# A sparsemax attention with its engine queues reordered, and a quantised convolutional layer whose weights are prepared during the projection before it

## The chip, the cores and the metric

The kernel runs on one NeuronCore of a Trainium2 chip. The metric is the device time of one execution in microseconds (us). Five engines work side by side, each with its own queue of instructions taken strictly in order: TensorE (PE in the profile, its weight loads PEld), VectorE (DVE), ScalarE (ACT), GpSimd (POOL) and SyncE (SP), which issues the DMAs. They wait for one another through semaphores that only count up.

## The reference, cut to what matters

Eight layers are applied to 2 x 512 tokens of 256 numbers. Two of them are touched.

```python
# layer "L0_ffn": quantised up projection, convolution over tokens, SiLU, quantised down projection
h = bit_linear(x, w1)                     # 256 -> 1024; x to 8 bits per token, w to -1, 0, 1 by mean|w|
h = depthwise_conv1d(h.transpose(0, 2, 1), conv_w, conv_b)   # 3 taps along the tokens
h = jax.nn.silu(h.transpose(0, 2, 1))
x = x + bit_linear(h, w2)                 # 1024 -> 256; h to 8 bits by its largest |value| per token

# layer "L1_xattn": 16 heads of 16, 512 queries, 1024 keys
scores = einsum('bhqd,bhkd->bhqk', qh, kh) * scale
attn = sparsemax(scores)                  # max(scores - tau, 0), tau such that a row sums to 1
out = einsum('bhqk,bhkd->bhqd', attn, vh)
```

## The kernel before, in words

The program is a row of stages. A stage is a block in which each engine has its own list of instructions; all engines meet at its end, so whatever ends last in a stage sets when the next begins.

**The projection of layer 0** (`project_out`, stage `l0o`) multiplies `o_all` by `wo` for eight token tiles (L324, 16 PE instructions a tile) and VectorE adds each tile to `x` (L337). ScalarE does nothing there.

**The convolutional layer** (`bit_conv_ffn`, stage `f0`) loads its weights at its own start (L2282 to L2285), sums their sizes on ScalarE (L2294, L2297), normalises and rounds `x` on VectorE (L2371 to L2399), takes the weight scales (L2403 to L2405) and rounds both weights (L2414 to L2416). Eight channel chunks follow, each one VectorE chain: widen by the token's scale (L2423, two halves), three taps (L2430, L2431, L2432), then SiLU on ScalarE (L2311). Then all eight token tiles are transposed and their largest values taken (L2349, L2436), the scales are spread over the partitions (L2442, L2354, L2315), the eight chunks are multiplied and rounded (L2448 to L2450), and only then the down products run (L2362) and are added (L2453).

**Sparse attention** (`sparse_attention`, stage `l1a`) works in 16 units of 8 rows; a row is 128 queries of a head against 1024 keys. For a unit `u`, in the order of the data:

- *candidate banks*: PE computes the scores once, a bank of 512 at a time (`first_row`, L1206, 16 banks a unit, two buffers); VectorE takes the 8 largest of each 128 (L1311).
- *threshold*: VectorE gets a first tau from the largest 8 (L1321 to L1330: running sums in 7 steps at L1326), then betters it in three rounds and counts once more (L1332 to L1338), and hands `minus_tau` to ScalarE (L1340) with a guess of the slope (L1341 to L1343).
- *first sums*: PE computes the scores again (`again`, L1216), ScalarE takes the excess over tau (L1483, eight rows). After them VectorE makes a step (`second_threshold`, L1349 to L1358), ScalarE sums again (L1497, "sums 1"), VectorE makes another (`third_threshold`, L1364 to L1372), ScalarE sums again ("sums 2").
- *settle*: VectorE takes the worst error (L1378 to L1382), PE turns it (`turn`, L1248), VectorE looks at it and branches (L1384 to L1408) and writes `shift` (L1412). PE turns `shift` (L1250), VectorE splits it (`cut`, L1418, L1420), SP places it by DMA.
- *probabilities*: PE computes the transposed scores, now with the shift in them (`second`, L1227, 8 tiles), ScalarE clips them (L1505), PE multiplies by the values (`value_products`, L1239), ScalarE copies the output (L1511).

The orders are written by hand. ScalarE's for a unit, with the probabilities of the unit before between its own sums:

```python
first_sums(u)                       # waits for tau_set(u) and settled(u-1)
for t in range(NC_):
    if u < UNITS and t == 2: sums(u, 1)
    if u < UNITS and t == 4: sums(u, 2)
    if u > 0: probabilities(u - 1, t)
if u > 0: copy_output(u - 1)
```

VectorE's is `cut(u-1)`, four rows of candidates of u+1, `second_threshold(u)`, four more rows, `third_threshold(u)`, the whole `first_threshold(u+1)`, `settle(u)`. PE's is in the printed code.

## Time and profile before

| what | value |
|---|---|
| median of 3 runs | 3362.21 us (3359.86 to 3367.62) |
| the profiled execution: its own time | 3360.47 us |
| its span, first to last instruction | 3358.5 us |
| instructions in the span | 37181 |
| mean granted TensorE clock | 0.843 of full speed |
| busy: PE, PEld, DVE, ACT, POOL | 2464.4, 1568.7, 2048.2, 1425.8, 423.8 us |

The span is the time on the chip between the first and the last instruction; 2.0 us lie around it. Busy time is an average over some twenty stages with different limits, so it does not say what a change in one stage is worth. The groups of rows below come from the timeline (instructions in order of time with the idle time of their engine before them and what ended it), from the groups by line, from a table of one tile, from the waits and from the windows.

### The profile page before, as it was taken

Reading aid. Unit: us, or ns where it says so; the run is one execution under the profiler, and the core shown is the slowest. Engines: PE = TensorE matmul, PEld = TensorE weight load, DVE = VectorE, ACT = ScalarE, POOL = GpSimd, SP = SyncE. Lnnn points to the kernel's source line nnn. Section 1 sums busy time; section 2 is a strip of 40 time slices with the busy share of each in tenths; the row PEclk is TensorE's granted clock in tenths of the full one; section 3 lists DMA queues with packets and bytes.
Section 4 is the critical chain, followed back from the end, with each engine's and each line's share of the span. In section 5 each row is a group of like instructions: output and inputs, shape, how many; then the busy total and the mean of one; then the engine's idle time right before and its main releaser. Section 6 shows DMA issues by size and latency. Waiting matters only on the chain. (4 is left out here: it accounts for less than half of the span.)

```text
span 3358.5 us, 37181 instructions
## 1 busy us (share of the span) xinstructions
PE 2464.4 (73%) x12065; PEld 1568.7 (47%) x12066; DVE 2048.2 (61%) x4901; ACT 1425.8 (42%) x2243; POOL 423.8 (13%) x228
## 2 busy tenths in 40 slices
PE   2999996355556566666499359997875996899598
PEld 1444444233233333324499336664435884444487
DVE  4666662856777777742466446775644555675477
ACT  1555551212778777881244122322441321366121
POOL 0000000001000000000577202111100211100021
PEclk8999998666777777776699789998887997799699
DMA  1001001125011111000466200002411112531010
GB/s 59 22 24 25 25 19 46 50 88 143 1 26 26 26 26 26 7 1 9 159 203 204 63 29 1 1 1 78 101 43 35 37 31 99 135 77 32 31 42 31
DMA packets 87789, 174.73 MB, mean 52 GB/s; under 512 B 23560, under 2 KB 52240, under 8 KB 84176
## 3 DMA queue, kind: packets, MB, share of 16 engines
q1 hardware_dynamic: 86096, 168.64, 17.3%
q0 software_dynamic: 1536, 4.20, 0.4%
...
## 5 line engine op out<-in xcount | busy, mean ns | idle before, releaser
L1497 ACT ACTIVATE l1a_over_s<-l1a_sc_s,l1a_minus_step_s 128x1024 bf16<-128x1024 f32 x256 | 290.0, 1140 | 3.5 <-DVE l1a_minus_step_s L1371 2.2
L1311 DVE MAX8 l1a_cand_s<-ps 128x8 f32<-128x128 f32 x1024 | 213.1, 281 | 68.8 <-PE ps L1206 65.1
L1239 PE MATMUL ps<-l1a_probs_s,l1h_v_s 128*32 128x256 f32 x1024 | 122.0, 564 | 159.1 <-ACT l1a_probs_s L1505 157.9
L1483 ACT ACTIVATE l1a_sc_s<-ps,l1a_minus_tau_s 128x1024 f32<-128x1024 f32 x128 | 142.0, 1113 | 137.5 <-DVE l1a_minus_tau_s L1340 53.0
L1024 DVE TENSOR_REDUCE l3a_shift_s<-ps 128x1 f32<-128x1024 f32 x128 | 150.2, 1218 | 50.8 <-PE ps L941 50.8
L1206 PE MATMUL ps<-l1h_ka_s,l1h_qa_s 128*128 128x512 f32 x256 | 132.3, 560 | 55.4 <-DVE l1a_cand_s L1311 45.0
L1085 ACT ACTIVATE l3a_probs_s<-ps 128x512 f32<-128x512 f32 x256 | 132.9, 602 | 89.0 <-PE ps L957 88.6
L1962 PE MATMUL ps<-m1e_x_part_s,m1e_up_part_s 128*128 128x256 f32 x1152 | 151.9, 290 | 13.9 <-POOL m1e_up_part_s L2142 12.3
L1962 PEld LDWEIGHTS ps<-m1e_x_part_s,m1e_up_part_s 128*128 128x128 f32 x1152 | 144.6, 196 | 17.4 <-POOL m1e_up_part_s L2142 15.4
L1505 ACT ACTIVATE l1a_probs_s<-ps 128x1024 f32<-128x1024 f32 x128 | 125.8, 1017 | 62.1 <-PE ps L1227 62.1
L646 ACT ACTIVATE l0a_probs_s<-ps 128x1024 f32<-128x1024 f32 x128 | 124.1, 1021 | 53.2 <-PE ps L482 51.7
L1227 PEld LDWEIGHTS ps<-l1h_qa_s,l1h_ka_s 128*128 128x128 f32 x512 | 96.9, 264 | 97.4 <-issue 63.4
L1227 PE MATMUL ps<-l1h_qa_s,l1h_ka_s 128*128 128x256 f32 x512 | 128.7, 390 | 17.1 <-ACT l1a_sc_s L1483 12.9
L566 DVE TENSOR_SCALAR l0a_probs_s<-l0a_probs_s 128x1024 f32<-128x1024 f32 x128 | 85.8, 690 | 71.4 <-ACT l0a_probs_s L646 70.4
L494 PE MATMUL ps<-l0a_probs_s,l0a_v_s 128*64 128x512 f32 x512 | 124.0, 605 | 0.0
L1216 PE MATMUL ps<-l1h_ka_s,l1h_qa_s 128*128 128x512 f32 x256 | 98.9, 496 | 30.2 <-ACT l1a_sc_s L1483 30.2
L1239 PEld LDWEIGHTS ps<-l1a_probs_s,l1h_v_s 128*32 128x32 f32 x1024 | 24.5, 133 | 206.1 <-ACT l1a_probs_s L1505 181.2
L1748 PE MATMUL ps<-m3e_x_part_s,m3e_up_part_s 128*128 128x512 f32 x432 | 102.5, 399 | 21.9 <-DVE m3e_x_part_s L1810 18.2
L2142 POOL TENSOR_TENSOR m1e_up_part_s<-m1e_up_s,m1e_up_part_s 128x1536 fp32r<-128x1536 f32 x30 | 105.2, 3507 | 69.5 <-ACT m1e_up_part_s L1996 69.5
L1748 PE MATMUL ps<-m2e_x_part_s,m2e_up_part_s 128*128 128x512 f32 x384 | 94.9, 404 | 23.2 <-DVE m2e_x_part_s L1810 12.2
L1206 PEld LDWEIGHTS ps<-l1h_ka_s,l1h_qa_s 128*128 128x128 f32 x256 | 58.4, 242 | 112.6 <-DVE l1a_cand_s L1311 100.5
L941 PE MATMUL ps<-l3h_ka_s,l3h_qa_s 128*128 128x512 f32 x256 | 97.2, 469 | 13.1 <-PEq L38 10.1
...
## 6 DMA issues: line engine op xcount, KB each, us to landing
...
```

Source lines behind the costliest of these rows:

```text
L646: nc.scalar.activation(probs[:, t % SLOTS, :], ps[:, 2 * (t % 2):2 * (t % 2) + 2, :].rearrange("p a n -> p (a n)"), ACT.Exp).then_inc(exp_ ...
L1024: nc.vector.reduce_max(shift[:, n % 2, rows * k:rows * k + rows], ps[:, 2 * (at % 2):2 * (at % 2) + 2, :].rearrange("p (r j) n -> p r (j n ...
L1085: nc.scalar.activation(probs[:, t % 2 * S + h, :], ps[:, 4 + i % 3, :], ACT.Exp).then_inc(exp_done, 1)
L1206: nc.tensor.matmul(ps[:, A0 + f % 2, :], qa[:, buf, h, at:at + P], ka[:, buf, h, j * BANK:(j + 1) * BANK], start=True, stop=True).then_inc ...
L1227: ins = nc.tensor.matmul(ps[:, PAIR + 2 * (place % 2) + h // 2, h % 2 * HALF:h % 2 * HALF + HALF], ka[:, buf, h, t * P:(t + 1) * P], qa[:, ...
L1239: ins = nc.tensor.matmul(ps[32 * h:32 * h + 32, VALUES, 0:HALF], v[:, n % 2, t, h, :], probs[:, t % 4, h * HALF:(h + 1) * HALF], start=(t ...
L1311: ins = nc.vector.max(cand[:, r, 8 * (c + j * 4):8 * (c + j * 4) + 8], ps[:, A0 + f % 2, c * P:(c + 1) * P])
L1483: nc.scalar.activation(sc[:, r, :], ps[:, PAIR + 2 * (place % 2):PAIR + 2 * (place % 2) + 2, :].rearrange("p a n -> p (a n)"), ACT.Relu, b ...
L1497: nc.scalar.activation(over[:, done % 2, :], sc[:, r, :], ACT.Relu, bias=minus_step[:, r:r + 1], accum_out=total[:, i, r:r + 1]).then_inc( ...
L1505: nc.scalar.activation(probs[:, t % 4, :], ps[:, PAIR + 2 * (place % 2):PAIR + 2 * (place % 2) + 2, :].rearrange("p a n -> p (a n)"), ACT. ...
L1748: ins = nc.tensor.matmul(ps[:, 2 * (u % 2) + way, :], up_parts[a][:, k, way, c, :], x_parts[b][:, k, half * BANK:(half + 1) * BANK], start ...
L1962: ins = nc.tensor.matmul(ps[:, u % 4, way * TOK:(way + 1) * TOK], up_parts[a][:, b % 2, k, way, c, :], x_parts[p][:, b % 2, k, :], start=( ...
```

## The change

In `sparse_attention`:

- PE: the candidate banks are issued one by one by a table. The first two of unit u+2 and the first two rows of `again` for u+1 are issued at the end of unit u. `turn` is split: `turn_worst` stands after the last `second` of the unit before, `turn_shift` after the two rows of `again`.
- VectorE: `first_threshold` is split. Its first part (`begin_threshold`) stands ahead of `third_threshold`, the guess of the slope after `settle`. `minus_tau` is handed over before the last count. The running sums take three wide steps instead of seven narrow ones, in two halves of a `best` tile with four zeros ahead of each row's eight values.
- ScalarE: both rounds of sums are cut into halves of four rows with tiles of probabilities between them.

In the convolutional layer:

- A new class `BitWeights` loads the weights, sums, scales and rounds them inside `project_out` of layer 0 (its argument `beside`), and the layer takes them from there.
- The first tap is a scaled copy on ScalarE; VectorE widens chunk c+1 before it convolves chunk c; the 1.8 us `memset` of all of `hid` becomes two narrow ones later.
- The second half goes by token tile: transpose (PE), largest value and scale (VectorE), scaled copy (ScalarE), rounding (VectorE), transpose back as bf16 (PE), copy (ScalarE), down product (PE), add (VectorE), one tile behind the other.

The program order on PE around the end of a unit (L1239 value products, L1216 and L1235 the scores again, L1206 and L1225 candidate banks, L1248 and L1267 the turn of the worst error, L1250 and L1271 the turn of the shift; L1227 and L1246 `second`). Before:

```order
L1227 MATMUL ps<-l1h_qa_s,l1h_ka_s 128x256 x4
L1239 MATMUL ps<-l1a_probs_s,l1h_v_s 32x256 x8
L1216 MATMUL ps<-l1h_ka_s,l1h_qa_s 128x512 x4
L1248 MATMUL ps<-ident,l1a_worst_s 1x128
L1250 MATMUL ps<-ident,l1a_shift_s 8x128
L1216 MATMUL ps<-l1h_ka_s,l1h_qa_s 128x512 x2
L1206 MATMUL ps<-l1h_ka_s,l1h_qa_s 128x512 x2
```

Now:

```order
L1246 MATMUL ps<-l1h_qa_s,l1h_ka_s 128x256 x4
L1267 MATMUL ps<-ident,l1a_worst_s 1x128
L1258 MATMUL ps<-l1a_probs_s,l1h_v_s 32x256 x4
L1235 MATMUL ps<-l1h_ka_s,l1h_qa_s 128x512 x2
L1225 MATMUL ps<-l1h_ka_s,l1h_qa_s 128x512 x2
L1258 MATMUL ps<-l1a_probs_s,l1h_v_s 32x256 x4
L1235 MATMUL ps<-l1h_ka_s,l1h_qa_s 128x512 x2
L1271 MATMUL ps<-ident,l1a_shift_s 8x128
```

The turn of the worst error moved ahead of the last two value products and of both rows of `again`; two candidate banks came in between.

VectorE between the second half of the candidates and the first round that betters tau. Before:

```order
L1364 TENSOR_SCALAR l1a_excess_s<-l1a_total_s 128x8
L1365 TENSOR_TENSOR l1a_slope_s<-l1a_excess_s 128x8
L1366 TENSOR_TENSOR l1a_slope_s<-l1a_slope_s,l1a_rstep_s 128x8
L1367 TENSOR_TENSOR l1a_slope_s<-l1a_slope_s,l1a_number_s 128x8
L1368 RECIPROCAL l1a_rcount_s<-l1a_slope_s 128x8
L1369 TENSOR_TENSOR l1a_slope_s<-l1a_excess_s,l1a_rcount_s 128x8
L1370 TENSOR_TENSOR l1a_step_s<-l1a_step_s,l1a_slope_s 128x8
L1371 TENSOR_SCALAR l1a_minus_step_s<-l1a_step_s 128x8
L1372 COPY l1a_rstep_s<-l1a_rcount_s 128x8
L1321 MAX l1a_best_s<-l1a_cand_s 128x8 x8
L1322 TENSOR_REDUCE l1a_last_s<-l1a_cand_s 128x8
L1326 TENSOR_TENSOR l1a_best_s<-l1a_best_s 128x8 x7
```

Now:

```order
L1340 MAX l1a_cand_s<-ps 128x8 x32
L1350 MAX l1a_best_s<-l1a_cand_s 128x8 x8
L1351 TENSOR_REDUCE l1a_last_s<-l1a_cand_s 128x8
L1356 TENSOR_TENSOR l1a_best_s<-l1a_best_s 128x8x8 x3
L1359 SCALAR_TENSOR_TENSOR l1a_best_s<-l1a_best_s,l1a_ranks_s 128x8x8
L1362 TENSOR_REDUCE l1a_tau_s<-l1a_best_s 128x8
L1408 TENSOR_SCALAR l1a_excess_s<-l1a_total_s 128x8
```

The eight-largest search and the running sums moved ahead of `third_threshold` (L1364, now L1408).

VectorE in the chunks of the convolutional layer. Before:

```order
L2423 TENSOR_TENSOR f_hid_s<-f_by_token_s,ps 128x512 x2
L2430 TENSOR_SCALAR f_conv_s<-f_hid_s,f_taps_s 128x1024
L2431 SCALAR_TENSOR_TENSOR f_conv_s<-f_hid_s,f_taps_s,f_conv_s 128x1024
L2432 SCALAR_TENSOR_TENSOR f_conv_s<-f_hid_s,f_taps_s,f_conv_s 128x1024
```

Now:

```order
L2549 TENSOR_TENSOR f_hid_s<-f_by_token_s,ps 128x512 x2
L2557 SCALAR_TENSOR_TENSOR f_conv_s<-f_hid_s,f0w_taps_s,f_conv_s 128x1024
L2558 SCALAR_TENSOR_TENSOR f_conv_s<-f_hid_s,f0w_taps_s,f_conv_s 128x1024
```

One instruction of 128x1024 per chunk left VectorE for ScalarE.

The diff, cut to its core:

```diff
@@ project_out(..., beside=None)
+                if beside is not None and t == 4:
+                    beside.total(pe)
                 if t >= 4:
                     pe.wait_ge(added, t - 3)
...
                 nc.vector.tensor_tensor(acc[:, t, :], acc[:, t, :], ps[:, t % 4, 0:D], ALU.add).then_inc(added, 1)
+                if beside is not None and t == 4:
+                    beside.scales(dve)
+                    beside.quantize(0)
+                if beside is not None and t == 5:
+                    beside.quantize(1)
@@ sparse_attention
+    SUMS = {2: (1, 0, 4), 3: (1, 4, 8), 5: (2, 0, 4), 6: (2, 4, 8)}
+    BESIDE_AGAIN = ((2, 2), (2, 2), (2, 3), (3, 4), (4, 5), (5, 7))
+    BESIDE_SECOND = {0: (7, 8), 1: (8, 9), 2: (9, 10), 3: (10, FIRST)}
...
             for u in range(UNITS + 1):
-                for r in range(ROWS):
-                    if u < UNITS:
+                if u < UNITS:
+                    for r in range(2, ROWS):
                         again(u, r)
-                    if r == 1 and u > 0:
-                        turn(u - 1)
-                    if u + 1 < UNITS and 2 <= r < 6:
-                        first_row(u + 1, r - 2)
+                        first_banks(u + 1, *BESIDE_AGAIN[r - 2])
                 if u == UNITS - 1:
                     denominators(0)
                 for t in range(NC_):
                     if u > 0:
                         second(u - 1, t)
-                    if u + 1 < UNITS and t < 4:
-                        first_row(u + 1, 4 + t)
+                    if t in BESIDE_SECOND:
+                        first_banks(u + 1, *BESIDE_SECOND[t])
...
+                    if t == NC_ - 1 and u < UNITS:
+                        turn_worst(u)
                     if u > 0 and t > 0:
                         value_products(u - 1, t - 1)
+                if u + 1 < UNITS:
+                    again(u + 1, 0)
+                    first_banks(u + 2, 0, 2)
                 if u > 0:
                     value_products(u - 1, NC_ - 1)
+                if u + 1 < UNITS:
+                    again(u + 1, 1)
+                if u < UNITS:
+                    turn_shift(u)
@@ sparse_attention, VectorE
                 second_threshold(u)
-                if u + 1 < UNITS:
+                if more:
                     for r in range(ROWS // 2, ROWS):
                         candidates(u + 1, r)
+                    begin_threshold(u + 1)
                 third_threshold(u)
-                if u + 1 < UNITS:
-                    first_threshold(u + 1)
+                if more:
+                    for i in range(MICHELOT):
+                        better_threshold(u + 1)
+                    hand_over(u + 1)
...
                 settle(u)
+                if more:
+                    guess_slope(u + 1)
@@ bit_conv_ffn, VectorE
+            widen(0)
+            for c in range(CH):
+                if c + 1 < CH:
+                    widen(c + 1)
+                convolve(c)
...
+            find_scale(0)
             for t in range(TQ):
+                if t + 1 < TQ:
+                    find_scale(t + 1)
+                make_whole(t)
+                if t >= 2:
+                    add(t - 2)
+            add(TQ - 2)
+            add(TQ - 1)
```

## Rows read from the trace of the kernel before

**Rows 1.** Table of the tile `l1a_shift_s`: durations, then first and last start
```profile
L1412 DVE TENSOR_TENSOR l1a_shift_s<-l1a_tau_s,l1a_step_s x16: 166/167/168, 853.7 to 1516.0; 128x8 f32<-128x8 f32 x16
```

**Rows 2.** Timeline of VectorE at a unit's end: start, duration, instruction, idle before
```profile
1094.20 0.17 DVE L1364 TENSOR_SCALAR l1a_excess_s<-l1a_total_s 128x8 f32<-128x8 f32 x1 [0.49 <-ACT l1a_over_s L1497]
...
1096.06 1.11 DVE L1321 MAX8 l1a_best_s<-l1a_cand_s 128x8 f32<-128x64 f32 x8 [0.17 <-DVE l1a_rstep_s L1372]
...
1097.38 1.43 DVE L1326 TENSOR_TENSOR l1a_best_s<-l1a_best_s 128x8 f32<-128x8 f32 x7
...
1099.36 0.69 DVE L1332 TENSOR_TENSOR l1a_above_s<-l1a_cand_s,l1a_tau_s 128x512 f32<-128x512 f32 x1
...
1110.42 0.17 DVE L1340 TENSOR_SCALAR l1a_minus_tau_s<-l1a_tau_s 128x8 f32<-128x8 f32 x1
...
1111.14 0.17 DVE L1378 TENSOR_SCALAR l1a_excess_s<-l1a_total_s 128x8 f32<-128x8 f32 x1
...
1113.49 0.28 DVE L1384 TENSOR_REDUCE l1a_worst_all_s<-ps 1x1 f32<-1x128 f32 x1 [1.60 <-PE ps L1248]
...
1115.09 0.17 DVE L1412 TENSOR_TENSOR l1a_shift_s<-l1a_tau_s,l1a_step_s 128x8 f32<-128x8 f32 x1 [1.14 <-DVEq L1408]
```

**Rows 3.** Timeline of ScalarE in the same unit: right after sums 2
```profile
1104.92 1.92 ACT L1505 ACTIVATE l1a_probs_s<-ps 128x1024 f32<-128x1024 f32 x2
```

**Rows 4.** Waits of the whole attention stage: total, times, longest
```profile
ACT l1a_sc_s L1483 <- PE ps L1216: 33.9, 58, 1.4
```

**Rows 5.** Timeline of PE: `again`, and value products in mid unit and after a pause
```profile
1068.35 1.20 PE L1216 MATMUL ps<-l1h_ka_s,l1h_qa_s 128*128 128x512 f32 x4
...
1090.33 0.64 PE L1239 MATMUL ps<-l1a_probs_s,l1h_v_s 128*32 128x256 f32 x8
...
1105.99 1.08 PE L1239 MATMUL ps<-l1a_probs_s,l1h_v_s 128*32 128x256 f32 x8 [8.33 <-ACT l1a_probs_s L1505]
```

**Rows 6.** Window of one unit: length, busy PE, PEld, DVE, ACT, POOL, clock, DMA
```profile
1071.60:1115.30 43.70, 25.27 (x130) 13.38 (x130) 31.93 (x132) 35.44 (x57) 1.80 (x1) 0.80 0.00 1
```

**Rows 7.** Timeline of VectorE: the last `shift` but one, and the last unit
```profile
1469.12 0.17 DVE L1412 TENSOR_TENSOR l1a_shift_s<-l1a_tau_s,l1a_step_s 128x8 f32<-128x8 f32 x1 [1.45 <-DVEq L1408]
...
1514.07 0.28 DVE L1384 TENSOR_REDUCE l1a_worst_all_s<-ps 1x1 f32<-1x128 f32 x1 [6.82 <-PE ps L1248]
```

**Rows 8.** Timeline of all engines, layer 0's projection and the convolutional layer
```profile
548.63 30.63 PE L324 MATMUL ps<-l0o_wo_s,l_o_all 128*128 128x256 f32 x128 [17.40 <-DMA l0o_wo_s<-l_wo]
...
580.72 1.77 DVE L2369 MEMSET f_hid_s<- 128x2056 f32 x1 [0.99 <-PEq L38]
...
585.95 0.17 DVE L2376 TENSOR_SCALAR f_var_eps_s<-f_mv_s 128x8 f32<-128x8 f32 x1
...
587.89 1.91 ACT L2294 ACTIVATE f_wabs_s<-f_w_s 128x2048 f32<-128x2048 f32 x1 [55.16 <-DMA f_cb_s<-f_cb]
...
591.94 1.28 ACT L2300 ACT_TABLE_LOAD   x1
...
593.48 0.20 DVE L2379 RECIPROCAL f_rstd_s<-f_dev_s 128x8 f32<-128x8 f32 x1 [7.36 <-ACT f_dev_s L2300]
...
607.37 1.29 DVE L2414 TENSOR_SCALAR f_w_s<-f_w_s,f_wscale_s 128x2048 f32<-128x2048 f32 x1
...
615.18 1.28 DVE L2423 TENSOR_TENSOR f_hid_s<-f_by_token_s,ps 128x512 f32<-128x512 f32 x2
...
654.93 1.15 ACT L2311 ACTIVATE f_act_t_s<-f_conv_s,f_cb_s 128x1024 f32<-128x1024 f32 x1 [3.83 <-DVEq L2433]
...
658.13 1.23 DVE L2436 TENSOR_REDUCE f_big_s<-ps 128x1 f32<-128x1024 f32 x1 [3.30 <-PE ps L2349]
...
706.71 0.48 DVE L2453 SCALAR_TENSOR_TENSOR x_rows<-ps,f_out_scale_s,x_rows 128x256 f32<-128x256 f32 x1 [0.39 <-PE ps L2362]
```

**Rows 9.** Groups of VectorE by line in the convolutional layer: busy, mean ns
```profile
L2430 DVE TENSOR_SCALAR f_conv_s<-f_hid_s,f_taps_s 128x1024 f32<-128x1024 f32 x8 | 6.0, 753 | 1.2 <-DVE f_hid_s L2423 0.2
...
L2449 DVE TENSOR_SCALAR f_tmp_s<-f_tmp_s 128x1024 f32<-128x1024 f32 x8 | 5.5, 693 | 0.3
```

379 lines of the change are left out of this document (232 added, 147 removed).

## The prediction

> **What bounds the kernel now.** I read the timeline stage by stage, because the kernel is a row of stages that each end at a meeting of all engines: a microsecond saved on what ends last in a stage comes off the total, one saved elsewhere does not. Nothing outside two stages is touched.
>
> The attention stage comes first. The table of the tile `shift` gives its rhythm [rows 1]: 16 settled units, the first at 853.7, the last at 1516.0, so 662.3 / 15 = 44.15 us a unit. Next the timeline of one unit, where the reader should ask of each engine what it waited for. VectorE starts `third_threshold` after 0.49 us of idleness ended by ScalarE [rows 2], so up to there ScalarE's sums lead. From 1094.20 on VectorE never waits for ScalarE again: `third_threshold` takes 1.86 us, the beginning of the next threshold 3.30 (1096.06 to 1099.36), three rounds and a count 11.06 (to 1110.42), hand-over and guess 0.72, and `settle` starts at 1111.14, or 39.5 after the unit's first sums. ScalarE had finished sums 2 at 1104.92 [rows 3], 6.2 us before. Second half: VectorE bounds. Then `settle` waits 1.60 us for PE's turn of the worst error and writes `shift` at 1115.09, 3.95 us after its start; the next first sums start 0.25 us later (timeline). ScalarE is busy 35.4 of 43.7 us [rows 6], so it is a floor well below.
>
> The convolutional layer runs from 580.72 to 707.2 [rows 8], and VectorE or the wait for the weights leads throughout: `rstd` waits 7.36 us for ScalarE, whose weight sums waited for the DMA until 587.89; the weights are rounded from 607.37 to 615.18; eight chunks take 654.93 - 615.18 = 39.75, or 4.97 each; the second half takes 51.1 us from the end of the last SiLU (656.1).
>
> **The change part by part: the attention.** For a unit, counted from the start of its first sums:
>
> - *First half.* Rows 0 and 1 of `again` are ready beforehand and the candidate banks are thinned among rows 2 to 7. ScalarE's waits for PE there are 33.9 / 16 = 2.1 us a unit [rows 4]; I let 1.6 go. Against it, sums 1 now have three tiles of probabilities ahead of their end instead of two, +0.96 (half of 1.92) [rows 3], and `second_threshold` stands behind a candidate bank that PE makes only beside the first `second`, so I charge +0.6. Sums 1 end about where they did (22.4).
> - *Begin ahead of third.* Its seven narrow steps of 0.204 become three wide ones. No row shows 128x64 with a stride of 12; between 0.17 (128x8) and 0.69 (128x512) [rows 2] I take 0.25, nearer the small end, so begin costs 3.30 - 1.43 + 0.75 = 2.6. It fills idleness only partly: candidates used to end 0.5 us before the sums. With the earlier banks they end about 1.5 earlier, so 2.6 - 0.5 - 1.5 leaves 0.6, and less where sums 1 come late; I charge +0.4. ScalarE has tiles 3 and 4 (1.9 us) to hide `third_threshold`.
> - *After third.* Three rounds and a count, 11.06, stay; begin (3.30) is gone and the guess of the slope (0.6) goes behind `settle`. `settle` starts 3.9 - 0.4 = 3.5 earlier: at 36.0 instead of 39.5. Sums 2, with one tile more before their end, finish near 34.3, so VectorE still leads by 1.7.
> - *Settle.* PE already stands at the turn when the worst error comes, so the 1.60 wait falls to 0.3: `shift` comes after 2.7, at 38.7.
> - *A new wait.* PE now holds the turn at its head for about 4 us. Queued behind it are the value products of tile 6, `again` row 0, two banks and tile 7; `copy_output` of the unit before waits for tile 7, and the first sums stand behind it on ScalarE. After such a pause PE is slow: eight value products took 1.08 us after 8.33 us of idleness and 0.64 in mid unit, at the upper of the two clock levels [rows 5]. A tile's eight passes start to start are thus 1.0 or 0.57, `again` 0.85 or 0.43 a row (four matmuls took 1.20 in a mixture), two banks 1.25 or 0.63. Chain: 36.5 + 0.15 + (1.0 + 0.85 + 1.25 + 1.0 = 4.1) + 0.3 + 0.38 (copy) = 41.4 slow; with 2.2 it is 39.5. I take 41.0, as the clock may rise on the way.
>
> So 41.0 against 43.96 for the first fourteen intervals (to 1469.12 [rows 7]; the last was 46.85): 14 x 2.96 = 41.4. The bounds are the fast chain (39.5: 14 x 4.46 = 62) and one in which begin is not hidden and the chain is slow (42.5: 20).
>
> The Trainium skill, "TensorE: Matmul & The Clock Gate", section "What's actually happening", says that the throttled state is the default and activity releases it. By that the chain runs at half speed in every unit and the sum is 14 x 2.6 = 36; with an always fast PE it would be 62. The rows after a pause bear it out.
>
> The first unit gains 3.6 (the same steps to `shift`) and 2.1 of start-up (0.7 of begin, and `minus_tau` handed over 1.4 before the count): -5.7. In the last unit the turn stood behind all probabilities, 6.82 us of waiting [rows 7]; that falls to 0.3, but two tiles more precede the end of sums 2 (+1.9) and the first sums start 2.2 after `shift`: -2.4. SP's placing moves with `shift`; its DMAs have some 8 us before `second` needs them. Attention: -41.4 - 5.7 - 2.4 = **-49.5** (bounds -28 and -70).
>
> **The convolutional layer.**
>
> - *Beside the projection.* Four more DMAs follow `wo` and its bias on SP. In the old place they landed 7.3 us after the first issue; here that is some 556, and the two sums on ScalarE take 4.05 [rows 8] (587.89 to 591.94): 560. PE reaches tile 4 at 548.63 + 4 x 3.45 = 562.4 and finds them done; the small product costs 0.5 (bounds 0 and 3.4, a tile's time, if the loads are late). VectorE has 3.0 us idle a tile; 0.6 + 3.8 after tile 4 and 3.8 after tile 5 (half of 7.81 each [rows 8]) make it late for tiles 5 and 6, and it has caught up at tile 7, for which the last add ends with PE. PE waits for add t-3 only, never behind the rounding.
> - *Start.* `memset` (1.8) leaves the front and the stage begins 0.5 later, so the variance is out at 586.1 - 1.8 + 0.5 = 584.8, and with ScalarE free and its table loaded before it waits, `rstd` comes 0.4 later: 585.2 instead of 593.48, **-8.3**. Two narrow memsets and a cast fill that wait. The Trainium skill, "ScalarE: Activation LUTs", section "What ACT_TABLE_LOAD costs", puts a switch at 2.66 us with its drain; by that 1.4 more would leave the path. The load here took 1.28 and the square root followed within 0.1 us [rows 8], so the trace disagrees and 1.28 stands.
> - *Rounding gone.* The chunks now wait for the spread scales, not the weights: transposes, spread and two copies end 18.1 us after `rstd` (timeline), at 603.35; before it was 21.7: **-3.5**.
> - *Chunks.* The first tap (0.75 [rows 9]) and a wait leave VectorE: 4.97 - 0.79 - 0.1 = 4.1 a chunk, **-7.1**. ScalarE's two instructions, 1.15 each (a SiLU of that size), fit; widening a chunk ahead covers the tap. If the tap took twice that they would still fit.
> - *Second half.* VectorE per tile: reduce 1.23 [rows 8], three small ones 0.6, rounding 2 x 0.69 [rows 9], two small 0.4, add 0.48, gaps 0.15: 4.24. ScalarE 2 x 1.15 and PE about 3 lie beside it. 8 x 4.24 = 33.9, plus 2.0 for the first transposes and 3.0 for the last tile's way through PE, ScalarE and PE: 38.9 against 51.1: **-12.2**. Should PE's slow clock set a tile's pace it is 42.
>
> Together -31.1 (bounds -25 and -34). A slot of 4 MB written by SP starts earlier and nobody waits for it.
>
> **Sum.** -49.5 - 31.1 = -80.6. The profiled execution took 3360.47, so 3279.9; the median lies 1.7 above it, so **3281.6**. A measurement of this kernel can tell 0.2% (6.7 us) from no change.
>
> **The rivals.**
>
> - *The new wait costs more* (15%). The banks 10 to 15 stand behind one `second`, and begin ahead of third is not hidden: a unit takes 42.5, attention -28, sum -59: 3303. For it: ScalarE led before third. Against: candidates already ended before the sums.
> - *PE is not slow after the turn* (13%): 39.5 a unit, -70 and -31: 3261. For it: more work stands right behind the turn. Against: eight passes took 1.08 after a pause.
> - *Slower* (4%). Halving the sums spreads PE's work thin, the clock stays at its lower level (1.2 GHz) for whole units and PE becomes the bound. Its work in a unit was 25.27 us at 0.80 [rows 6], or 40.4 at 0.5; with its two pauses of 4 us (between halves of sums 2, and at the turn) a unit is 48. 14 x 4.04 = +57, first and last unit -8, the layer -31: +18, or 3380. It decides from 46.7 us a unit. Against: the first twenty microseconds of a unit are as dense as before.
> - *The reorder does nothing* (2%): VectorE's work is the same and another wait takes the place. The layer alone: 3331.
>
> **How the numbers follow.** The forecast has 66% and a range of its own from 3269 to 3298 (a unit 40.3 to 41.8, the layer -34 to -26). The asked range also takes in the two neighbours with half of that spread: 3256 to 3309. Faster: 66 + 15 + 13 + 2 = 96%, of which I hold back 1% for no change; slower 4%.
>
> **What would show it.** `shift` every 41 us; `copy_output` right before the first sums, both waiting for PE's value products; the wait for the turn of the worst error near 0.3; VectorE without idleness from third to settle; `rstd` of the layer at 585, first chunk at 603, 4.1 us a chunk, 4.2 a tile. Wrong if units are longer than 42, if PE waits in layer 0's projection for the weight sums, or if ScalarE waits for VectorE between its sums by more than 1 us.

## The result, and the profile after the change

| what | before | after |
|---|---|---|
| median | 3361.03 us (3359.69 to 3367.62, 4 runs) | 3256.02 us (3251.34 to 3258.62, 4 runs) |
| profiled execution, its own time | 3360.47 us | 3251.34 us |
| its span | 3358.5 us | 3249.6 us |
| mean granted TensorE clock | 0.843 | 0.854 |

The ratio is 0.9682, with a 95% interval of 0.9665 to 0.9699: 105 us less between the medians, where 81 were forecast. The parts of the change moved the time the way the prediction gave; the first half of an attention unit and the second half of the layer gave more than forecast.

I compared the two traces at the meetings of the stages. VectorE's first instruction of the attention stage comes at 780.84 before and 746.89 after; its first instruction behind the stage at 1574.72 and 1472.07. The attention took 793.9 us and takes 725.2 (-68.7, forecast -49.5). The layer's stage begins at 580.7 and 580.4, and the first DMA of the next stage is issued at 707.68 and 672.16 (-35.5, forecast -31.1). By the end of the attention the two executions stand 102.65 us apart. Behind it nothing was changed; the distance wanders between 102.6 and 109.4 us and is 108.9 at the end. The profiled execution of after is also 4.7 us below its median, so I put what lies between -102.65 and -105 to no part of the change.

**The unit.** The table of the tile `shift` of the changed kernel, which answers to [rows 1]:

```profile
L1456 DVE TENSOR_TENSOR l1a_shift_s<-l1a_tau_s,l1a_step_s x16: 166/168/170, 814.6 to 1411.9; 128x8 f32<-128x8 f32 x16
```

The last but one stands at 1370.54: (1370.54 - 814.62) / 14 = 39.71 us a unit, where 43.96 was before and 41.0 forecast. The last interval is 41.33 (46.85 before).

VectorE in a settled unit, timeline (start, duration, instruction, idle before), answering to [rows 2]:

```profile
1036.28 0.17 DVE L1408 TENSOR_SCALAR l1a_excess_s<-l1a_total_s 128x8 f32<-128x8 f32 x1 [0.39 <-ACT l1a_over_s L1552]
...
1049.14 0.17 DVE L1422 TENSOR_SCALAR l1a_excess_s<-l1a_total_s 128x8 f32<-128x8 f32 x1
...
1050.18 0.28 DVE L1428 TENSOR_REDUCE l1a_worst_all_s<-ps 1x1 f32<-1x128 f32 x1 [0.28 <-PE ps L1267]
...
1051.76 0.17 DVE L1456 TENSOR_TENSOR l1a_shift_s<-l1a_tau_s,l1a_step_s 128x8 f32<-128x8 f32 x1 [1.13 <-DVEq L1452]
```

The first sums of this unit start at 1014.62 (next fence). `third_threshold` starts 21.66 after them, still behind an idle time of 0.39, so the 2.6 us of begin ahead of it are hidden. `settle` starts at 34.52 (39.5 before, 36.0 forecast), the wait for the turn is 0.28 (0.3 forecast), and `shift` comes 2.62 after `settle` (2.7 forecast).

ScalarE in the same unit:

```profile
1014.34 0.38 ACT L1566 ACTIVATE l_o_all<-ps 128x256 f32<-128x256 f32 x1 [4.35 <-PE ps L1258]
1014.62 1.11 ACT L1538 ACTIVATE l1a_sc_s<-ps,l1a_minus_tau_s 128x1024 f32<-128x1024 f32 x1
...
1023.32 2.11 ACT L1560 ACTIVATE l1a_probs_s<-ps 128x1024 f32<-128x1024 f32 x2
1026.09 1.15 ACT L1552 ACTIVATE l1a_over_s<-l1a_sc_s,l1a_minus_step_s 128x1024 bf16<-128x1024 f32 x1 [0.66 <-DVE l1a_minus_step_s L1400]
...
1036.07 1.91 ACT L1560 ACTIVATE l1a_probs_s<-ps 128x1024 f32<-128x1024 f32 x2
```

And the two rows that bound the eight first sums in the kernel before, which the prediction did not lay side by side:

```profile
1071.62 1.11 ACT L1483 ACTIVATE l1a_sc_s<-ps,l1a_minus_tau_s 128x1024 f32<-128x1024 f32 x1 [2.75 <-DVE l1a_shift_s L1412]
...
1083.16 1.96 ACT L1505 ACTIVATE l1a_probs_s<-ps 128x1024 f32<-128x1024 f32 x2
```

Eight first sums took 11.54 us and take 8.70, which is eight rows of 1.09 with nothing between them. (Over the thirteen settled units they took 10.5 to 12.7; now they take 8.7 in ten of them and 9.5 in three.) Sums 1 end 21.45 after the start of the first sums, 22.44 before. Of the 2.84 us won, 0.66 go again in the wait for `second_threshold` shown above: VectorE's candidates had waited 1.66 us for a bank of PE's (at 1019.17), so it comes to that step late.

PE behind the last `second` of the unit, answering to [rows 5]:

```profile
1049.70 0.37 PE L1267 MATMUL ps<-ident,l1a_worst_s 128*1 128x128 f32 x1 [3.94 <-DVEq L1425]
1050.00 1.08 PE L1258 MATMUL ps<-l1a_probs_s,l1h_v_s 128*32 128x256 f32 x8
1051.01 1.22 PE L1235 MATMUL ps<-l1h_ka_s,l1h_qa_s 128*128 128x512 f32 x2
1052.04 1.05 PE L1225 MATMUL ps<-l1h_ka_s,l1h_qa_s 128*128 128x512 f32 x2
1053.02 1.08 PE L1258 MATMUL ps<-l1a_probs_s,l1h_v_s 128*32 128x256 f32 x8
```

This is the new wait, as forecast: 3.94 us at the turn, then four pieces of about 1.0 each, then `copy_output` (at 1054.17) and the first sums. From the turn's start to the copy it is 4.47 us (4.55 in the prediction's slow sum). The granted clock of this window, and of the unit:

```profile
1010.00:1014.00 4.00, 4.00 (x21) 1.57 (x20) 1.10 (x7) 0.00 (x0) 0.00 (x0) 0.50 0.00 0
1014.60:1054.50 39.90, 27.65 (x131) 13.66 (x131) 31.13 (x128) 34.88 (x59) 0.31 (x1) 0.71 0.00 1
```

At the end of the unit before (the same passes, 1010 to 1014) the clock is 0.50, the lower of its two levels (1.2 GHz), with PE busy without a break. The prediction's hope ("the clock may rise on the way") came true in part: in five of the fourteen unit ends before the last, tile 7 already runs at the upper level (2.4 GHz), and the first sums come about 0.4 us sooner after `settle`. One of the five (the clock is 0.50 until 973, 0.67 in the next microsecond, 1.00 from 974):

```profile
973.59 0.65 PE L1258 MATMUL ps<-l1a_probs_s,l1h_v_s 128*32 128x256 f32 x8
```

By "TensorE: Matmul & The Clock Gate" in the Trainium skill, section "What's actually happening", the throttled level is the default and activity releases it. The trace agrees: each chain starts at the lower level after the pause and the level rises behind it, in the unit shown only after tile 7 (0.69 from 1014 to 1015, then 1.00).

Waits of the attention stage (total, times, longest), answering to [rows 4]; five waits are left of 58, all before the second unit's first sums are through, one of them, 5.5 us long, right behind the first `shift`:

```profile
ACT l1a_sc_s L1538 <- PE ps L1235: 6.4, 5, 5.5
```

**The layer**, timeline of VectorE and ScalarE, answering to [rows 8]:

```profile
557.63 1.91 ACT L2322 ACTIVATE f0w_wabs_s<-f0w_w_s 128x2048 f32<-128x2048 f32 x1 [24.77 <-DMA f0w_cb_s<-f_cb]
...
579.45 0.42 DVE L346 TENSOR_TENSOR x_rows<-x_rows,ps 128x256 f32<-128x256 f32 x1 [0.99 <-PE ps L333]
...
580.36 1.28 ACT L2419 ACT_TABLE_LOAD   x1 [18.69 <-PEq L38]
...
584.34 0.19 DVE L2518 RECIPROCAL f_rstd_s<-f_dev_s 128x8 f32<-128x8 f32 x1
...
601.61 2.72 DVE L2549 TENSOR_TENSOR f_hid_s<-f_by_token_s,ps 128x512 f32<-128x512 f32 x4 [4.12 <-ACT f_by_token_s L2426]
...
635.08 1.15 ACT L2401 ACTIVATE f_act_t_s<-f_conv_s,f0w_cb_s 128x1024 f32<-128x1024 f32 x1 [1.37 <-DVE f_conv_s L2558]
...
650.90 1.22 DVE L2570 TENSOR_REDUCE f_big_s<-ps 128x1 f32<-128x1024 f32 x1
...
654.77 1.21 DVE L2570 TENSOR_REDUCE f_big_s<-ps 128x1 f32<-128x1024 f32 x1
...
671.22 0.48 DVE L2589 SCALAR_TENSOR_TENSOR x_rows<-ps,f_out_scale_s,x_rows 128x256 f32<-128x256 f32 x1 [0.39 <-PE ps L2463]
```

The projection's last add starts at 579.45 (579.30 before), 24.33 after its first (24.10 before): the preparation beside it costs 0.2 us. `rstd` is at 584.34 (-9.1; forecast -8.3), the first widening 17.3 after it, the last SiLU at 635.08, a tile of the second half takes 3.87 (4.24 forecast), and 35.5 us pass from the end of the last SiLU to the end of the last add (38.9 forecast, 51.1 before).

### The profile page after: what moved, and what is told of

Same layout as the page of the kernel before. It is cut to its first block and busy times, and to the rows that moved or that the text cites. A ratio compares the mean times of both kernels' runs of the same rounds, so it can differ in the third digit from the quotient of the medians.

```text
span 3249.6 us, 37333 instructions
## 1 busy us (share of the span) xinstructions
PE 2455.1 (76%) x12114; PEld 1555.4 (48%) x12114; DVE 2023.2 (62%) x4851; ACT 1443.0 (44%) x2265; POOL 423.8 (13%) x228
## 5 line engine op out<-in xcount | busy, mean ns | idle before, releaser
L1225 PE MATMUL ps<-l1h_ka_s,l1h_qa_s 128*128 128x512 f32 x256 | 133.1, 533 | 39.8 <-DVE l1a_cand_s L1340 26.9
L2015 PEld LDWEIGHTS ps<-m1e_x_part_s,m1e_up_part_s 128*128 128x128 f32 x1152 | 144.5, 196 | 17.3 <-POOL m1e_up_part_s L2195 15.4
L660 ACT ACTIVATE l0a_probs_s<-ps 128x1024 f32<-128x1024 f32 x128 | 124.1, 1021 | 53.2 <-PE ps L496 51.6
L1235 PE MATMUL ps<-l1h_ka_s,l1h_qa_s 128*128 128x512 f32 x256 | 111.2, 523 | 36.6 <-ACT l1a_sc_s L1538 32.5
L1560 ACT ACTIVATE l1a_probs_s<-ps 128x1024 f32<-128x1024 f32 x128 | 126.2, 1013 | 21.7 <-PE ps L1246 21.2
L1246 PEld LDWEIGHTS ps<-l1h_qa_s,l1h_ka_s 128*128 128x128 f32 x512 | 92.3, 246 | 66.6 <-issue 45.3
L1246 PE MATMUL ps<-l1h_qa_s,l1h_ka_s 128*128 128x256 f32 x512 | 118.6, 367 | 4.2 <-DMA l1h_qa_s<-l1a_minus_lo_s 4.2
L1848 ACT ACTIVATE m2e_h_s<-ps,m2ew_b_s 128x512 f32<-128x512 f32 x64 | 44.0, 688 | 137.6 <-PE ps L1801 125.1
L1038 DVE TENSOR_REDUCE m2a_shift_s<-ps 128x2 f32<-128x1024 f32 x64 | 75.1, 1219 | 45.7 <-PE ps L955 45.7
```

What stands on the lines that cost most here:

```text
L660: nc.scalar.activation(probs[:, t % SLOTS, :], ps[:, 2 * (t % 2):2 * (t % 2) + 2, :].rearrange("p a n -> p (a n)"), ACT.Exp).then_inc(exp_ ...
L1038: nc.vector.reduce_max(shift[:, n % 2, rows * k:rows * k + rows], ps[:, 2 * (at % 2):2 * (at % 2) + 2, :].rearrange("p (r j) n -> p r (j n ...
L1225: nc.tensor.matmul(ps[:, A0 + f % 2, :], qa[:, buf, h, at:at + P], ka[:, buf, h, j * BANK:(j + 1) * BANK], start=True, stop=True).then_inc ...
L1246: ins = nc.tensor.matmul(ps[:, PAIR + 2 * (place % 2) + h // 2, h % 2 * HALF:h % 2 * HALF + HALF], ka[:, buf, h, t * P:(t + 1) * P], qa[:, ...
L1560: nc.scalar.activation(probs[:, t % 4, :], ps[:, PAIR + 2 * (place % 2):PAIR + 2 * (place % 2) + 2, :].rearrange("p a n -> p (a n)"), ACT. ...
L2015: ins = nc.tensor.matmul(ps[:, u % 4, way * TOK:(way + 1) * TOK], up_parts[a][:, b % 2, k, way, c, :], x_parts[p][:, b % 2, k, :], start=( ...
```

## The experiments

Each is the changed kernel with one edit, unless it says otherwise. Times are medians of 4 runs; where a ratio stands it is to the kernel before on the same chip in the same hour, and is to be held against the changed kernel's 0.9682. "A unit" is the mean of the first fourteen intervals of `shift`.

**1. The layer's part alone** (the attention as before).

> The convolutional layer's part of the change alone, with the attention as before. Stages add up: the layer gave 35.5 us in the trace of the changed kernel (from the first issue of the stage after it), so this runs 35 us below the kernel before, about 3326, and its layer has rstd 8 to 9 us earlier, 4.2 us a chunk and 3.9 us a tile in the second half. Rival, the terms of the prediction (rstd 8.3, first chunk 3.5, chunks 7.1, second half 12.2): 31 us, 3330. Second rival: what the changed kernel gained beyond the two stages (105 us between medians) belongs to the layer: 38 us or more, 3323 or less.

Measured: 3323.13 us, ratio 0.9895 (0.9878 to 0.9911), or 35 us less. The interval reaches from 30 to 41 us, so the time alone does not part the theory from its rivals (31, or 38 and more); the trace does. In it a chunk takes 4.18 and a tile 3.87, and from the projection's last add to the first DMA of the next stage it is 93.1 us, against 92.7 in the changed kernel and 128.4 before: 35.2 of the layer. The theory holds.

**2. The attention's part alone** (the layer as before).

> The attention's part alone, with the layer as before. Theory: the attention stage took 793.9 us before and 725.2 changed, so this runs 69 us below the kernel before, about 3292, with a shift every 39.7 us; with the layer's 35.5 it makes 104 of the 105 between the medians. Rival: the two parts touch (the clock or the transfers stand otherwise after an earlier layer), and this gives under 60 or over 75 us.

Measured: 3289.84 us, ratio 0.9795 (0.9778 to 0.9811), or 69 us less; a unit is 39.71. The product of both ratios is 0.9692, the changed kernel's is 0.9682, a difference well inside their intervals: the parts add up, and no effect of one on the other shows.

**3. The candidate banks in their old places.**

```diff
-    BESIDE_AGAIN = ((2, 2), (2, 2), (2, 3), (3, 4), (4, 5), (5, 7))
-    BESIDE_SECOND = {0: (7, 8), 1: (8, 9), 2: (9, 10), 3: (10, FIRST)}
+    BESIDE_AGAIN = ((0, 2), (2, 4), (4, 6), (6, 8), (8, 8), (8, 8))
+    BESIDE_SECOND = {0: (8, 10), 1: (10, 12), 2: (12, 14), 3: (14, FIRST)}
...
-                    first_banks(u + 2, 0, 2)
```

> The changed kernel with its candidate banks back in the places of before (two behind each of rows 2 to 5 of the scores again, two behind each of the first four tiles of second, none at a unit's end); rows 0 and 1 of the scores again stay early. Theory: the thin table is what freed the first sums (11.54 us in a unit before, 8.70 now), so they wait for PE again by 1.5 to 2.8 us, sums 1 end that much later, VectorE's third_threshold with them, and a unit takes 41.2 to 42.5 instead of 39.7: 3277 to 3295. Rival: the two rows ahead alone do it (PE is then ahead of ScalarE by two rows for the whole of the first sums), and the time stays within 3256 to 3263.

Measured: 3281.85 us, ratio 0.9769 (0.9752 to 0.9785): 29 us more than with the thin table; a unit is 41.61. Its timeline, PE, ScalarE and VectorE in one unit (the first sums start at 1024.56):

```profile
1028.66 0.51 PE L1225 MATMUL ps<-l1h_ka_s,l1h_qa_s 128*128 128x512 f32 x1 [0.29 <-DVE l1a_cand_s L1338]
...
1029.68 1.11 ACT L1536 ACTIVATE l1a_sc_s<-ps,l1a_minus_tau_s 128x1024 f32<-128x1024 f32 x1 [0.63 <-PE ps L1235]
...
1047.08 1.91 ACT L1558 ACTIVATE l1a_probs_s<-ps 128x1024 f32<-128x1024 f32 x2
...
1049.62 0.17 DVE L1406 TENSOR_SCALAR l1a_excess_s<-l1a_total_s 128x8 f32<-128x8 f32 x1
```

Here is how banks reach ScalarE. The second bank of a pair waits for VectorE to empty a buffer; the row of the scores stands behind it, and ScalarE behind the row. The first sums take 10.5 us instead of 8.7. And the candidates, begun later, end later: `third_threshold` now follows the end of sums 1 by 2.5 us (1.2 to 1.7 in most units), begin is no longer hidden. That is what the prediction's first rival feared, begin no longer hidden, but by another way: the rival had banks 10 to 15 behind one `second` as its cause, and with them there, in the changed kernel, begin stays hidden.

**4. Begin behind `third_threshold` again.**

```diff
-                    begin_threshold(u + 1)
                 third_threshold(u)
                 if more:
+                    begin_threshold(u + 1)
                     for i in range(MICHELOT):
                         better_threshold(u + 1)
```

> The changed kernel with the beginning of the next threshold back behind third_threshold. Theory: ahead of it those 2.6 us lie wholly in VectorE's wait for sums 1 (0.39 us of idleness are even left), so behind it they come on top of VectorE's second half: third_threshold 0.2 to 0.4 earlier, settle 2.2 to 2.4 later, a unit 42.0 instead of 39.7: 3288 (3284 to 3292). Rival, the prediction's term (0.4 of begin is not hidden) with ScalarE's second half as a new bound: 3284 or less. Second rival: the shorter path of the turn hides it, 3262 or less.

Measured: 3296.69 us, ratio 0.9802 (0.9785 to 0.9818): 40 us more; a unit is 42.46. VectorE in a unit whose first sums start at 1029.61:

```profile
1051.26 0.17 DVE L1408 TENSOR_SCALAR l1a_excess_s<-l1a_total_s 128x8 f32<-128x8 f32 x1 [2.88 <-ACT l1a_over_s L1552]
...
1066.88 0.17 DVE L1422 TENSOR_SCALAR l1a_excess_s<-l1a_total_s 128x8 f32<-128x8 f32 x1
```

`third_threshold` is where it was (21.65 after the first sums) behind 2.88 us of idleness, and `settle` is 37.27 after them instead of 34.52: the move is worth its whole 2.75 us, more than the 2.2 to 2.4 I gave (and the time is above my range), because third gains nothing from its absence.

**5. Whole rounds of sums.**

```diff
-    SUMS = {2: (1, 0, 4), 3: (1, 4, 8), 5: (2, 0, 4), 6: (2, 4, 8)}
+    SUMS = {2: (1, 0, 8), 4: (2, 0, 8)}
```

> The changed kernel with whole rounds of sums as before (sums 1 before tile 2, sums 2 before tile 4). Theory: sums 1 end 0.96 us earlier, but VectorE's begin ends at 21.3 after the first sums and holds third_threshold, so at most 0.3 a unit is gained: 3252 to 3257, no difference. Rival A: with sums in one piece PE has no place for tiles and falls behind in second and the banks, a unit gets longer by over 0.5: 3263 or more. Rival B, by the prediction's +0.96 for the third tile: third_threshold comes that much earlier, a unit 0.9 shorter: 3244 or less.

Measured: 3269.54 us, ratio 0.9725 (0.9709 to 0.9741): 15 us more; a unit is 40.92. My theory was wrong, rival A right. ScalarE and VectorE at the end of a unit:

```profile
1056.43 1.02 ACT L1560 ACTIVATE l1a_probs_s<-ps 128x1024 f32<-128x1024 f32 x1 [1.42 <-PE ps L1246]
...
1058.59 1.02 ACT L1560 ACTIVATE l1a_probs_s<-ps 128x1024 f32<-128x1024 f32 x1 [1.14 <-PE ps L1246]
1058.88 0.28 DVE L1428 TENSOR_REDUCE l1a_worst_all_s<-ps 1x1 f32<-1x128 f32 x1 [2.87 <-PE ps L1267]
```

With sums 2 in one piece the last four tiles come one behind the other, and PE, at its lower clock after a pause of 7.15 us, needs 2.16 us a tile (1.01 of value products, 1.15 of `second`) where ScalarE needs 0.95. The turn stands behind the last `second`, so `settle` waits 2.87 us. Halving the sums gives PE's slow tiles a place; that is its use here. Sums 1 do end sooner, but VectorE's begin holds `third_threshold`, which comes 21.2 after the first sums instead of 21.66: 0.5 won, and more than that lost at the end.

**6. The turn of the worst error in its old place.**

```diff
-                    if t == NC_ - 1 and u < UNITS:
-                        turn_worst(u)
...
                 if u + 1 < UNITS:
                     again(u + 1, 1)
                 if u < UNITS:
+                    turn_worst(u)
                     turn_shift(u)
```

> The changed kernel with the turn of the worst error moved back behind the last value products and the second row of the scores again. Theory: PE then does tile 6's products in its pause and tile 7, the row and the banks behind it at the lower clock (1.0 each), and the turn comes at about 54.2 where it came at 49.7: shift 4.3 later, and as the first sums now follow shift by 0.27 instead of 2.7, they come 1.9 later: a unit 41.6, 3283. Rival: the place of the turn does not matter, as PE has the same work between the last probabilities and the first sums: 3253 to 3260. Second rival: the copy of the output, earlier by 1.1, is what counts and the time falls.

Measured: 3293.4 us, ratio 0.9795 (0.9779 to 0.9812): 38 us more; a unit is 42.35. `settle` waits where it did before the change, only longer:

```profile
1064.65 0.17 DVE L1421 TENSOR_SCALAR l1a_excess_s<-l1a_total_s 128x8 f32<-128x8 f32 x1
...
1069.00 0.28 DVE L1427 TENSOR_REDUCE l1a_worst_all_s<-ps 1x1 f32<-1x128 f32 x1 [3.60 <-PE ps L1267]
```

The theory's mechanism holds, but a unit is 0.7 longer than I worked out. The trace has most of the rest. `shift` comes 5.9 to 7.3 us after `settle` instead of 2.6 to 2.9, and the next first sums follow it by 0.25 instead of 1.9 to 2.7. And `settle` itself comes later: the first sums stand right behind `shift` now, PE is still at the lower clock for their rows, and they take 9.3 to 10.0 us instead of 8.7 (`settle` 35.0 to 35.5 after their start, 34.5 before the edit). That I had left out.

**7. The weights prepared in the layer again**, one execution.

> The changed kernel with the weights of the convolutional layer loaded, summed, scaled and rounded inside the layer again, the rest of the layer as changed. Theory: rstd waits for ScalarE's sums of the weights again and comes at 593.4 instead of 584.3 in the trace, and of the 7.8 us of rounding 4.4 are not covered by transposes and copies: the first widening at about 615, +13.5 in all, 3269 to 3270. Rival, the prediction's terms (8.3 and 3.5): 3268. Second rival: the projection loses what the layer gains and the time stays at 3256 to 3258.

Measured: 3268.91 us in one execution. VectorE:

```profile
592.83 0.20 DVE L2508 RECIPROCAL f_rstd_s<-f_dev_s 128x8 f32<-128x8 f32 x1 [10.23 <-ACT f_dev_s L2407]
...
616.54 1.29 DVE L2542 TENSOR_TENSOR f_hid_s<-f_by_token_s,ps 128x512 f32<-128x512 f32 x2 [2.15 <-PE ps L2475]
```

The first widening comes 14.9 later than in the changed kernel (up to 2.15 of it because in this edit PE's first product waits for both roundings). The first `shift` is 14.2 later. This execution was 1.6 us ahead at the projection's first add (executions whose projection is the same differ there by more), so counted from that add it is 16.5. A single time does not part the theory (3269 to 3270) from the prediction's terms (3268): four executions of the changed kernel lie between 3251.34 and 3258.62. It does exclude the second rival, that the projection loses what the layer gains.

**8. The first tap on VectorE**, one execution.

```diff
-                dve.wait_ge(tapped, c + 1)
+                own.link(nc.vector.tensor_scalar(y, v[:, :, 0:NQ], taps[:, c, 0:1], None, ALU.mult))
```

> The changed kernel with the first tap of the convolution back on VectorE. Theory: VectorE sets a chunk's pace (4.18 us with nothing between its instructions but 0.1 us), so a chunk takes 4.18 + 0.75 = 4.93 to 4.97 again and the last SiLU comes 6 us later: about 3262. Rival: with the tap on ScalarE a chunk is set by the way over two engines, and VectorE alone is as fast: 3256 to 3257, a chunk under 4.5.

Measured: 3256.57 us in one execution (the changed kernel's executions lie between 3251.34 and 3258.62), which cannot decide. The trace can:

```profile
618.40 1.28 DVE L2545 TENSOR_TENSOR f_hid_s<-f_by_token_s,ps 128x512 f32<-128x512 f32 x2
...
623.34 1.29 DVE L2545 TENSOR_TENSOR f_hid_s<-f_by_token_s,ps 128x512 f32<-128x512 f32 x2
```

A chunk takes 4.94 instead of 4.18. The first reduce behind the chunks comes at 644.66 instead of 638.35, and the first widening had come 0.16 later: the tap is worth 6.15 us there. No run takes back the second half by token tile, the layer's largest term; it is read from the two traces alone.

**9. The running sums in seven narrow steps**, one execution.

```diff
-                for i, by in enumerate((1, 2, 4)):
...
+                for j in range(5, 12):
+                    own.link(nc.vector.tensor_tensor(best[:, 0, :, j], best[:, 0, :, j], best[:, 0, :, j - 1], ALU.add))
```

> The changed kernel with the running sums in seven narrow steps instead of three wide ones. Theory: begin grows by 1.43 - 0.74 = 0.69 us and VectorE has 0.39 us of idleness left before third_threshold, so a unit grows by 0.3 (39.7 to 40.0): +4, about 3260. Rival: the wide steps are on the path in full: 0.7 a unit, 3266. Second rival: hidden altogether: 3256.

Measured: 3259.42 us in one execution, which again cannot decide; in the trace a unit is 40.14, and in a unit whose first sums start at 1015.95 `third_threshold` starts at 1038.10 without idleness, 22.15 after them (21.66 with wide steps). Near the theory's 0.3: of the 0.69 us that the wide steps save, 0.4 to 0.5 is on the path.

**10. The output sooner**, a first try at a better order on PE.

```diff
-                    if t == NC_ - 1 and u < UNITS:
-                        turn_worst(u)
                     if u > 0 and t > 0:
                         value_products(u - 1, t - 1)
+                if u < UNITS:
+                    turn_worst(u)
+                if u > 0:
+                    value_products(u - 1, NC_ - 1)
                 if u + 1 < UNITS:
                     again(u + 1, 0)
+                    again(u + 1, 1)
                     first_banks(u + 2, 0, 2)
```

> The changed kernel with another order on PE at a unit's end: value products of tile 6, the turn of the worst error, value products of tile 7, both rows of the scores again, two banks, the turn of the shift. Theory: what ends last in a unit is tile 7's value products, the copy of the output behind them and the next first sums; in a typical unit shift is written 2.4 us before the copy starts. One row of the scores again (1.0) and two banks (1.0) no longer stand ahead of tile 7, and tile 6 stands ahead of the turn where PE would be idle: the first sums come 1.7 to 2.0 us earlier, a unit 37.8 instead of 39.7, 14 x 1.9 = 27: 3229 (3225 to 3238). Rival: the later banks and the later turn (up to 0.4 us behind tile 6) are waited for by VectorE, whose chain already leads in the second half, and under 7 us are left: 3249 or more.

Measured: 3233.79 us, ratio 0.9624 (0.9608 to 0.964): 19 us less than the changed kernel; a unit is 38.16. End of a unit:

```profile
1042.97 0.38 ACT L1565 ACTIVATE l_o_all<-ps 128x256 f32<-128x256 f32 x1 [1.61 <-PE ps L1258]
...
1043.58 0.17 DVE L1455 TENSOR_TENSOR l1a_shift_s<-l1a_tau_s,l1a_step_s 128x8 f32<-128x8 f32 x1 [1.13 <-DVEq L1451]
...
1044.18 1.11 ACT L1537 ACTIVATE l1a_sc_s<-ps,l1a_minus_tau_s 128x1024 f32<-128x1024 f32 x1 [0.82 <-PE ps L1235]
```

The copy now comes 0.6 ahead of `shift`. I had overlooked that the row of the scores, now behind tile 7, is waited for too. In the last unit the turn behind tile 6 costs 2 us (interval 43.37).

**11. The count behind `settle`**: PE's turn first, then tiles 6 and 7, both rows, two banks; and on VectorE

```diff
                 nc.vector.tensor_scalar(minus_tau[:, k, :], tau[:, k, :], -1.0, None, ALU.mult).then_inc(tau_set, 1)
-                count_above(u)
...
                 settle(u)
                 if more:
+                    count_above(u + 1)
                     guess_slope(u + 1)
```

> A version meant to beat both kernels. The changed kernel with PE's order: turn of the worst error, value products 6 and 7, both rows of the scores again, two banks, turn of the shift; and on VectorE the last count above tau (1.44 us) moved behind settle, where VectorE waits for PE's turn of the shift. Theory: settle then starts when ScalarE's sums 2 end, 33.4 after the first sums instead of 34.5; tile 6's products start at 34.35, tile 7's end at 36.4, the first row again is there at 37.4, shift at 36.1: a unit 37.5 instead of 39.71 (output_sooner had 38.16), the last unit as in the changed kernel: 3225 (3221 to 3230), or 0.9595 of the kernel before. Rival: the candidates, begun 1.3 later behind the count, hold second_threshold or third_threshold and give it back: 38.2 a unit or more, 3234.

Measured: 3222.35 us, ratio 0.9587 (0.9571 to 0.9603), so 32 us below the changed kernel by the ratios (1%); a unit is 37.66. The run changes two things at once, PE's order and the place of the count, and what each is worth is not parted. VectorE and ScalarE at the end of a unit whose first sums start at 1001.82, and two windows of the same unit:

```profile
1035.32 0.17 DVE L1420 TENSOR_SCALAR l1a_excess_s<-l1a_total_s 128x8 f32<-128x8 f32 x1 [0.23 <-ACT l1a_over_s L1552]
...
1038.30 0.38 ACT L1566 ACTIVATE l_o_all<-ps 128x256 f32<-128x256 f32 x1 [1.20 <-PE ps L1258]
1039.51 1.11 ACT L1538 ACTIVATE l1a_sc_s<-ps,l1a_minus_tau_s 128x1024 f32<-128x1024 f32 x1 [0.82 <-PE ps L1235]
```

```profile
1010.00:1020.00 10.00, 8.49 (x52) 4.53 (x53) 9.62 (x51) 9.26 (x16) 0.00 (x0) 1.00 0.01 2
...
1024.00:1040.00 16.00, 10.76 (x57) 5.37 (x58) 13.00 (x37) 13.98 (x23) 1.68 (x1) 0.50 0.00 1
```

`settle` starts as soon as sums 2 end (33.5), the count fills VectorE's wait for the turn of `shift`, and what ends last is again PE at the lower clock: tiles 6 and 7 and one row, from 1036.2 to 1039.5.

**12. PE's pauses filled**, on top of 11: ten products of 128x384 that nobody reads ahead of tile 3's and tile 5's products and ahead of the turn.

```diff
+                    if 0 < u < UNITS and t in (4, 6, 7):
+                        fill_pause(u - 1)
```

> count_behind with PE's three long pauses in a unit (3.9 us before tile 3's products, 2.0 before tile 5's, 2.8 before the turn) each filled by ten products of 128x384 whose result nobody reads. Theory: PE's clock falls in the first of these pauses (in count_behind the granted clock is 1.00 up to 1020 and 0.50 from 1024 to 1040), and the first sums then wait for tile 6's and 7's products and a row of the scores at that level (3.0 us, 1.6 at the upper one). With the pauses filled the clock stays up, shift leads again, the first sums follow it by 0.3 and a unit takes 36.8 instead of 37.66: 3222 - 12 = 3210 (3207 to 3214). Rival A: the clock falls all the same, the thirty products take 4 us a pause and hold the turn: 38.5 a unit or more, 3234. Rival B: what is waited for after the turn is not a matter of the clock: within 3219 to 3225.

Measured: 3218.67 us, ratio 0.9579 (0.9564 to 0.9595), against 0.9587 without: the intervals overlap, and the theory's 3207 to 3214 was missed. (Rival B's 3219 to 3225 is as near, but its reason is refuted below.) A unit is 37.43 on average, but the units differ: four lie between 36.40 and 37.05, ten between 37.3 and 38.0. Three windows of a long unit, then PE and ScalarE behind the turn of a long and of a short one:

```profile
1017.00:1021.00 4.00, 4.00 (x21) 3.09 (x21) 3.62 (x20) 4.00 (x7) 0.00 (x0) 0.59 0.00 0
1021.00:1033.00 12.00, 7.96 (x60) 5.63 (x58) 10.74 (x28) 12.00 (x21) 0.00 (x0) 1.00 0.01 1
...
1033.00:1037.00 4.00, 3.17 (x19) 1.31 (x20) 1.95 (x9) 2.34 (x5) 0.82 (x1) 0.62 0.01 2
```

```profile
884.39 0.64 PE L1258 MATMUL ps<-l1a_probs_s,l1h_v_s 128*32 128x256 f32 x8
...
886.73 1.12 ACT L1546 ACTIVATE l1a_sc_s<-ps,l1a_minus_tau_s 128x1024 f32<-128x1024 f32 x1 [0.34 <-PE ps L1235]
...
1034.10 1.99 PE L1258 MATMUL ps<-l1a_probs_s,l1h_v_s 128*32 128x256 f32 x16
...
1037.36 1.11 ACT L1546 ACTIVATE l1a_sc_s<-ps,l1a_minus_tau_s 128x1024 f32<-128x1024 f32 x1 [0.82 <-PE ps L1235]
```

In this unit the clock falls before the first filler (0.59 from 1017 to 1021, behind six candidate banks with 0.3 us of waiting for VectorE between them) and is back at 1.00 from 1021 to 1033, where number 11 had 0.50 from 1024 to 1040. But the fillers end 2.0 us before the turn, and in most units the clock falls again there. In three unit ends it does not: eight value products take 0.64, and the first sums follow `shift` by 0.4 to 0.8 instead of 1.2 to 1.65. (The fourth short unit is the first, which has no output of a unit before to wait for.) So the price of the slow passes is shown in single units, about as the theory had it; holding the clock for all units was not achieved, and a longer filling was not tried.

## Why the prediction had the mechanism right and its sum too small

- *Forecast 3281.6, measured 3256.0*, on the lower edge of the range. The mechanism was as told, new wait included; the attention gave 19 us more and the layer 4.4 more.
- *The new wait.* "PE is slow after the turn" is right: 0.50 is the clock in the window shown, and `settle` to `copy_output` took 5.03 us (the prediction's slow sum has 5.05). Taking 41.0 instead of its 41.4, for a clock that rises on the way, was too hopeful: it rises in five of fourteen unit ends and gives 0.4 us there, about 0.15 a unit. The rival with the fast chain had nearly the right attention (-70) for the wrong reason.
- *First half: the step that failed.* "ScalarE's waits for PE there are 2.1 us a unit; I let 1.6 go." The first sums became 2.84 us shorter. The wait table counts only what it names a wait; the gaps between rows (1072.72 to 1074.02 is 1.30 for a row that needs 1.09) come on top. Laying eight rows of 1.09 beside the 11.54 they took would have shown 2.8. And 0.5 was kept back for no row. That is 1.2 a unit. The other two charges of this step were right: 0.66 for `second_threshold` (0.6), 0.90 for one tile more ahead of the end of sums 1 (0.96); the first two tiles stand 0.25 longer than before. So sums 1 end 1.0 sooner, where the prediction had them "about where they did".
- *Begin ahead of third.* Its own price was right (2.6 us, 0.25 a wide step). "I charge +0.4" was wrong: nothing of it shows (experiment 4: the whole 2.75 is hidden). `third_threshold` starts 0.92 sooner than before where +0.4 was charged, and from there to `settle` 4.08 is gone where 3.9 was forecast. Together they bring `settle` from 36.0 to 34.5 (0.92, 0.4 and 0.18), which with the slow chain gives 39.7 to 39.9: measured 39.71. Over fourteen units this is the missing 18 us.
- *First and last unit.* -5.1 for the first (-5.7 forecast). The last interval fell by 5.5, and 1.4 came back behind it: -4.1 for -2.4. I have not followed that term further.
- *Slower, by the clock.* The unit's mean clock did fall, from 0.80 to 0.71, but not for the whole unit as that rival had it: it is 1.00 from 1014.6 to 1030, falls by 1034 and is 0.50 from there to the end. PE was busy for 27.65 of 39.9 us; outside the chain behind the turn I found its work waited for only in the first half, where the 0.66 us at `second_threshold` come from.
- *The projection.* 0.5 charged, 0.2 seen: loads landed by 557.6, the sums were done at 561.7, and PE's small product came at 565.2 (562.4 was forecast for its turn, too early as the first tile takes longer than the 3.45 us of the others).
- *Start of the layer.* `rstd` -9.1 for -8.3: the variance is out at 583.99 and not at 584.8, as the stage does not begin later than before (580.40). The table load runs from 580.36, while VectorE still takes the statistics, and is off the path as forecast. So what a switch costs did not matter here. The Trainium skill ("ScalarE: Activation LUTs", section "What ACT_TABLE_LOAD costs") has 1.28 us for the load, as this trace has, and some 1.38 us of drain on top, 2.66 in all; the drain does not show, neither here nor in the kernel before, where the load at 591.94 follows a sum that ended at 591.93 and `rstd` starts at 593.48. First widening 17.3 after `rstd` for 18.1. Together -13.6 for -11.8.
- *Chunks.* 4.18 each for 4.1; from the first widening to the last SiLU 33.47 for 39.75 before, -6.3 for -7.1. The tap's 6.15 (experiment 8) is nearly all of it.
- *Second half.* 35.5 for 38.9, because a tile takes 3.87 for 4.24. I had added durations. Three small instructions take 0.46 from the first's start to the next wide one (0.15 to 0.17 long each, 0.19 apart, and an instruction that waits for none of them starts 0.07 after the last), where I had 0.6; the add gives way to the next reduce after 0.40 of its 0.48, and no gap is left for which I had 0.15.
